# Window attention: value products of both rows at once, own half picked by two projection products; maxima turned in V's bank; V ahead of fc2

## The chip, the core and the metric

The kernel is one program on one core of a Trainium2 chip, whose engines run side by side and meet only at semaphores: TensorE (PE in the rows; PEld is its weight loads), VectorE (DVE), ScalarE (ACT), GpSimd (POOL) and SyncE (SP), which issues DMAs. The metric is device time in microseconds (us) for one execution. All arithmetic is float32.

## The reference, cut to what matters

The input is x of (4, 16, 512, 512). Layer 0 is a block of window attention with an MLP, layer 1 ten steps of a surface flow, layers 2 and 3 two residual pairs of 3x3 convolutions. The change touches layer 0 alone:

```python
x = x + depthwise_conv3x3(x, pos_w) + pos_b            # 16 channels
y = affine(x)                                          # windows of 8x8 = 64 tokens
q, k, v = split(y @ qkv_w.T + qkv_b)                   # 2 heads of 8 channels
out = softmax(q * 8 ** -0.5 @ k.T) @ v
x = x + (out @ proj_w.T + proj_b)
x = x + gelu(affine2(x) @ fc1_w.T + fc1_b) @ fc2_w.T + fc2_b
```

## The kernel before

`attention_stage` does layer 0 and is over before the other layers begin. It cuts the image into 256 **chunks**. A chunk is 8 window rows of 16 channels, which fill the 128 partitions, by 8 windows (WC) of 64 tokens (N), so its main tiles are 128 x 512. Two neighbouring window rows are a **row group** of 32 partitions; there are four (RG), and r is 0 or 1 for the row inside one.

The stage is software-pipelined over slots: one function `slot` on each engine issues, in an order written out by hand, the work of the chunks i-3 to i+2. Each engine runs its own copy in order and waits at semaphores. TensorE's loop holds 20 slots (`every_slot(pe, slot, 5)`), those of ScalarE and VectorE hold 4. One slot of TensorE, with the lines of the profile:

- `scores` of chunk i, first half of the windows (L204), 16 products into the four banks `ps_w`. It waits for `exp_done`: ScalarE must have read the previous contents with its second exponential (L354).
- `values` of chunk i-1, row groups 0 and 1 (L247). For every window, row r and row group one product writes 32 rows by 64 columns of `ps_o`. The stationary operand is `vx`, in which the other row's columns are zero, so that the two products of r = 0 and 1 add up in the same place: 32 products in a call, two calls in a slot.
- `project` of chunk i-2 (L319): one 128 x 512 product with the block-diagonal `w_proj` into bank 0 of `ps_mm`.
- `scores`, second half (L204), which waits for VectorE's first maximum (L483); `values`, row groups 2 and 3.
- `fc1` of chunk i-2 (L275), which waits for the second maximum (L483) because it overwrites `ps_w`.
- `turn_max` (L214): a transpose of the maxima into a bank of its own, `ps_t`; VectorE copies it out (L491). Then `sums` (L260), the denominators.
- `turned`, first half (L228, L234): transposed scores less their maxima. `query` (L283) and `key` (L289) of chunk i+1 into banks 1 and 0 of `ps_mm`. `turned`, second half, which waits for ScalarE's first exponential.
- `fc2` of chunk i-2 (L310) into bank 0, once ScalarE has read the key there (L373); last `value` of chunk i+1 (L298), 16 products into bank 1.

ScalarE's slot is: copy V to `vx` (L386), the output rows (L415), a table load (L423), gelu of i-2 (L404), a table load (L425), logarithm and exponential for the reciprocals (L395, L397), exponential of half 0 (L354), split of Q (L363) and K (L373), exponential of half 1 (L354). VectorE's slot is: maximum of half 0 (L483), `residual` (L508), maximum of half 1, two convolution taps (L469), the copy of the maxima (L491), two more taps and their end (L475), `divide` of i-1 (L500: `ps_o` times the reciprocals into `o_sb`), the first five taps of the next chunk (L464, L469), `finish` of i-2 (L517).

A product stands in the trace as two matmul records and two weight loads.

Of the kernel before, what the change touches and what calls it, by code (L numbers as in the profile page):

```python
# [11 lines left out]
ALU = mybir.AluOpType  # L12
ACT = mybir.ActivationFunctionType
# [4 lines left out]
def attention_stage(nc, x, dst, wt, DST_PAD=2):  # L18

    P = 128  # L20
# [15 lines left out]
    with ExitStack() as ctx:  # L36
        def sb(n, shape):
            return ctx.enter_context(nc.sbuf_tensor("att_" + n, shape, F32))
# [4 lines left out]
        def psum(n, shape):  # L43
            return ctx.enter_context(nc.psum_tensor("att_" + n, shape, F32))
# [3 lines left out]
        qkv_raw, qkv_al = sb("qkv_raw", [P, 3, P]), sb("qkv_al", [P, 3, P])  # L48
        fc1_raw, fc1_al = sb("fc1_raw", [P, RG, P]), sb("fc1_al", [P, RG, P])
        w_qkv, w_fc1 = sb("w_qkv", [P, 3, P]), sb("w_fc1", [P, RG, P])  # L50
        w_proj, w_fc2 = sb("w_proj", [P, P]), sb("w_fc2", [P, RG, P])
        ident = sb("ident", [P, P])
        vec = sb("vec", [P, 24])
        pos_w, pos_b = vec[:, 0:9], vec[:, 9:10]
# [8 lines left out]
        xs = sb("xs", [P, 4, T])  # L63
        qx = sb("qx", [P, 2, WC, 2, N])
        kx = sb("kx", [P, 2, WC, HEADS, N])
        vx = sb("vx", [P, 2, 2, WC, RG, 2, HEADS, HD])
        mx = sb("mx", [P, RG, 32])
        mx_t = sb("mx_t", [P, P])
        minus = sb("minus", [P, WC, P])
# [1 line left out]
        pick = sb("pick", [P, 2, P // RG])  # L71
        rec = sb("rec", [P, T])
        b_out = sb("b_out", [P, 1])
        o_sb = sb("o", [P, T])
        x2 = sb("x2", [P, 2, T])
        hid = sb("hid", [P, 2, RG, T])
        y_sb = sb("y", [P, T])
        out_rows = sb("out_rows", [P, 2, WS, 2 * CW])

        ps_w = psum("w", [P, RG, T])  # L80
        ps_t = psum("t", [P, T])[:, 0:P]
        ps_o = psum("pv", [P, T])
        ps_mm = psum("m", [P, 2, T])
        ps_m = [ps_mm[:, k, :] for k in range(2)]

        w_in, setup, w_made, w_ready = sem("w_in"), sem("setup"), sem("w_made"), sem("w_ready")
# [14 lines left out]
        def wait(eng, s, value):  # L101

            if not isinstance(value, int) or value > 0:
                eng.wait_ge(s, value)
# [16 lines left out]
        def after(eng, *users):  # L121

            for s, c in users:
                if there(c):
                    eng.wait_ge(s, c + 1)
                    return
# [47 lines left out]
        def _(pe):  # L174
# [8 lines left out]
                pe.matmul(ps_mm[:, 0, k:k + 1], qkv_raw[:, k, :], beta1, start=True, stop=True)  # L183
            pe.matmul(ps_mm[:, 0, 3:4], fc1_raw[:, 0, :], beta2, start=True, stop=True).then_inc(w_made, 1)
            pe.wait_ge(w_ready, 1)
            pe.matmul(ps_mm[:, 0, 4:5], w_proj[:, :], b_qkv[:, 2:3], start=True, stop=True).then_inc(w_made, 1)
            pe.wait_ge(w_ready, 2)

            WH = WC // 2
# [18 lines left out]
            def turn_max(i):  # L208

                if not there(i):  # L210
                    return
                pe.wait_ge(max_done, i * 2 + 2)
                wait(pe, mx_copied, i)
                pe.transpose(ps_t[:, :], mx[:, :, :].rearrange("p g k -> p (g k)"), ident[:, :]).then_inc(mx_turned, 1)  # L214

            def turned(i, par, half):
# [20 lines left out]
            def values(i, par, p):  # L237
                if not there(i):
                    return
                if p == 0:  # L240
                    pe.wait_ge(exp_done, i * 2 + 2)
                    pe.wait_ge(v_split, i + 1)
                    wait(pe, o_done, i)
                for w in range(WC):
                    for r in range(2):
                        for rg in (2 * p, 2 * p + 1):
                            mm = pe.matmul(ps_o[32 * rg:32 * rg + 32, w * N:(w + 1) * N],  # L247
                                           vx[:, par, r, w, rg].rearrange("p a h d -> p (a h d)"),
                                           pt[:, par, rg, w, r * N:(r + 1) * N], start=(r == 0), stop=(r == 1))
                mm.then_inc(pv_made[p], 1)  # L250

            def sums(i, par):
# [25 lines left out]
            def query(i, turn4):  # L278
                if not there(i):
                    return  # L280
                pe.wait_ge(conv_step, (i + 1) * STEPS_OF_CONV)
                after(pe, (v_split, i - 1))
                pe.matmul(ps_m[1], w_qkv[:, 0, :], xs[:, turn4, :], start=True, stop=True).then_inc(q_made, 1)  # L283

            def key(i, turn4):
# [17 lines left out]
            def fc2(i, par):  # L303

                if not there(i):
                    return
                pe.wait_ge(gelu_done, i + 1)
                after(pe, (k_split, i + 3), (rec_made, i + 1), (x2_done, i))
                for j in range(RG):
                    mm = pe.matmul(ps_mm[32 * j:32 * j + 32, 0, :], w_fc2[:, j, 32 * j:32 * j + 32], hid[:, par, j, :],  # L310
                                   start=True, stop=True)
                mm.then_inc(f2_made, 1)

            def project(i):
                if not there(i):
                    return
                pe.wait_ge(o_done, i + 1)
                after(pe, (y_done, i - 1), (k_split, i + 2))
                pe.matmul(ps_m[0], w_proj[:, :], o_sb[:, :], start=True, stop=True).then_inc(proj_made, 1)  # L319

            def slot(i, turn4):
                par = turn4 % 2
                o = 1 - par
                scores(i, par, 0)
                values(i - 1, o, 0)
                project(i - 2)
                scores(i, par, 1)
                values(i - 1, o, 1)
                fc1(i - 2, par)
                turn_max(i)  # L330
                sums(i - 1, o)
                turned(i, par, 0)
                query(i + 1, (turn4 + 1) % 4)
                key(i + 1, (turn4 + 1) % 4)
                turned(i, par, 1)
                fc2(i - 2, par)
                value(i + 1, (turn4 + 1) % 4)

            every_slot(pe, slot, 5)

# [1 line left out]
        def _(act):  # L342
# [34 lines left out]
            def split_v(i, par):  # L377
                if not there(i):
                    return
                act.wait_ge(v_made, i + 1)  # L380
                wait(act, pv_made[1], i - 1)
                for h in range(HEADS):
                    hp = slice(N * h, N * h + N)
                    vp = ps_mm[hp, 1, :].rearrange("p (w g r d) -> p w g r d", w=WC, g=RG, r=2)
                    for r in range(2):
                        last = act.activation(vx[hp, par, r, :, :, r, h, :], vp[:, :, :, r, :], ACT.Copy)  # L386
                last.then_inc(v_split, 1)

            def reciprocals(i):
# [44 lines left out]
        @block.vector  # L434
        def _(dve):
            dve.memset(mx[:, :, :], 0.0)
            dve.memset(vx[:].rearrange("p a b c d e f g -> p (a b c d e f g)"), 0.0).then_inc(setup, 1)
            dve.wait_ge(w_in, 16 * 9)
            dve.tensor_scalar(qkv_al[:, :, :], qkv_raw[:, :, :], alpha1, None, ALU.mult)
            dve.tensor_scalar(fc1_al[:, :, :], fc1_raw[:, :, :], alpha2, None, ALU.mult).then_inc(setup, 1)  # L440
# [52 lines left out]
            def divide(i):  # L493
                if not there(i):
                    return
                dve.wait_ge(rec_made, i + 1)
                dve.wait_ge(pv_made[0], i + 1)
                dve.wait_ge(pv_made[1], i + 1)
                wait(dve, proj_made, i)
                dve.tensor_tensor(o_sb[:, :], ps_o[:, :], rec[:, :], ALU.mult).then_inc(o_done, 1)  # L500

            def residual(i, par, turn4):

# [32 lines left out]
def attention_weights(a):  # L536

    import numpy as np
    C, WR, HID = 16, 8, 64
    f = np.float32  # L540

    def blocks(m):

        i, o = m.shape
        z = np.zeros((WR, i, WR, o), m.dtype)
        for r in range(WR):
            z[r, :, r, :] = m
        return z.reshape(WR * i, WR * o)

    def tile(v):  # L550
        return np.tile(np.asarray(v).reshape(-1), 128 // np.asarray(v).size).reshape(128, 1)

    qkv = a["qkv_w"]
    p = np.arange(128)
    row = (p // C) % 2
    head = (p // (C // 2)) % 2
    scale = (C // 2) ** -0.5
    vec = np.concatenate(
        [np.tile(a["pos_w"].reshape(C, 9), (WR, 1)), tile(a["pos_b"]), tile(a["alpha1"]), tile(a["beta1"]), tile(a["alpha2"]),
         tile(a["beta2"])] + [tile(a["qkv_b"][C * k:C * k + C]) for k in range(3)] +  # L560
        [tile(a["proj_b"]), tile(a["fc1_b"]), tile(a["fc2_b"])] +
        [np.where(row == r, scale, 0).astype(f).reshape(128, 1) for r in range(2)] +
        [np.where(head == h, 1, 0).astype(f).reshape(128, 1) for h in range(2)], axis=1).astype(f)
    fc2 = blocks(np.ascontiguousarray(a["fc2_w"].T)).reshape(WR * HID // 128, 128, 128).transpose(1, 0, 2)
    return dict(
        color=np.stack([blocks(a["color1"]), blocks(a["color2"])], axis=1),
        qkv=np.stack([blocks(np.ascontiguousarray(qkv[C * k:C * k + C].T)) for k in range(3)], axis=1),
        fc1=blocks(np.ascontiguousarray(a["fc1_w"].T)).reshape(128, 4, 128),
        proj=blocks(np.ascontiguousarray(a["proj_w"].T)),
        fc2=np.ascontiguousarray(fc2),  # L570
        ident=np.eye(128, dtype=f),
        minus=np.where((p % 32)[:, None, None] == 2 * np.arange(8)[None, :, None] + (p // 64)[None, None, :], -1, 0).astype(f),
        pick=np.stack([(((p[:, None] // 64) == (np.arange(32) // 8) % 2) & (np.arange(32) // 16 == r)).astype(f)
                       for r in range(2)], axis=1),
        vec=vec)
# [855 lines left out]
```

## Time and profile before

| | us |
|---|---|
| median of 3 runs | 28650.5 (28632.8 to 28668.2) |
| the profiled execution | 28647.7, its span 28645.9 |
| attention stage | from the start to about 5250 |
| TensorE busy over the whole span | 26744.7 (93%) |

The attention stage is the first seven of the forty slices of the page; after it come the surface flow and the convolutions, which the change leaves alone. A merged line of a timeline gives the start, the duration from the first to the last of its instructions, how many there are, and in brackets the idle time of the engine ahead of it with what ended it. The end of a matmul is modelled, so starts are the surer numbers.

### The profile page before, as it was taken

What the parts mean: (1) busy time and instruction counts of PE and PEld (TensorE: products, weight loads), DVE (VectorE), ACT (ScalarE), POOL (GpSimd) and SP (SyncE); (2) the same over time, 40 slices, a digit from 0 to 9 for tenths busy, and PEclk for the clock granted to TensorE, in tenths of its full rate; (3) what the DMA queues carried; (4) which work ended last, traced back from release to release, by engine and by line L of the source; (5) the groups of instructions that cost most, each with busy time, mean ns of one, the idle gap of its engine ahead of it and who ended that gap; (6) DMA issues with size and microseconds to landing.
All of it is one profiled execution on the core that took longest, in us unless ns stands there. A gap on an engine that the chain in (4) does not pass through costs nothing. (4 is left out here: it accounts for less than half of the span.)

```text
span 28645.9 us, 827717 instructions
## 1 busy us (share of the span) xinstructions
PE 26744.7 (93%) x334232; PEld 12655.2 (44%) x334232; DVE 23740.9 (83%) x26151; ACT 23103.3 (81%) x23277; POOL 8975.8 (31%) x9524
## 2 busy tenths in 40 slices
PE   8999999999989989998999899999989998999799
PEld 5666666444334433443434344334434443444455
DVE  6666666799989989998999899889989998999222
ACT  6666666799989989998999899889989998999111
POOL 0000000244434434443444344434434443444000
PEclk9999999999999999999999999999999999999899
DMA  1111111699999999999999999999999999999654
GB/s 33 32 32 32 32 32 32 126 176 176 178 177 176 177 177 178 176 176 178 176 176 178 178 176 176 180 175 176 176 178 175 176 176 179 176 176 176 119 106 90
DMA packets 1942097, 4147.74 MB, mean 145 GB/s; under 512 B 590960, under 2 KB 722544, under 8 KB 1938160
## 3 DMA queue, kind: packets, MB, share of 16 engines
q0 software_dynamic: 1196800, 3565.77, 70.6%
q1 hardware_dynamic: 701424, 469.69, 8.2%
q10 hardware_dynamic: 41088, 67.14, 1.1%
q8 instruction: 2726, 44.66, 0.6%
q14 instruction: 59, 0.48, 0.0%
HBM read 294.41 MB, written 201.33 MB: 17 GB/s over the span
## 5 line engine op out<-in xcount | busy, mean ns | idle before, releaser
L872 PE MATMUL surf_ps<-surf_u,surf_matf 64*64 64x512 f32 x184960 | 20141.9, 593 | 1129.8 <-ACT surf_pq L895 703.1
L872 PEld LDWEIGHTS surf_ps<-surf_u,surf_matf 64*64 64x64 f32 x184960 | 8316.3, 133 | 12956.2 <-issue 12897.1
L929 ACT ACTIVATE surf_p2q<-surf_pq 128x2048 f32<-128x2048 f32 x1360 | 2599.9, 1912 | 1484.5 <-DVE surf_pq L1016 1484.5
L969 POOL DMA_DIRECT2D surf_u<-surf_ds x4080 | 3458.4, 1156 | 954.0 <-issue 483.3
L962 POOL DMA_DIRECT2D surf_p2q<-surf_p2q x1360 | 1161.3, 854 | 7773.6 <-DVE surf_Ha L1038 7280.0
L956 POOL DMA_DIRECT2D surf_nK<-surf_B x1360 | 1236.4, 909 | 6884.4 <-ACT surf_B L933 6870.3
L1051 DVE SCALAR_TENSOR_TENSOR surf_rH<-surf_Hc,surf_dt_ab,surf_rH 128x1024 f32<-128x1024 f32 x1360 | 1744.0, 1282 | 1454.7 <-DMA surf_Hc<-surf_m 1045.0
L981 POOL DMA_DIRECT2D surf_Hc<-surf_Ha x1360 | 2187.1, 1608 | 351.2 <-DVE surf_Hc L1060 344.2
L975 POOL DMA_DIRECT2D surf_Hc<-surf_m x1360 | 1466.2, 1078 | 1648.1 <-DMA surf_Hc<-surf_Ha 1521.8
L1027 DVE SCALAR_TENSOR_TENSOR surf_nK<-surf_Ac,surf_Cc 128x1024 f32<-128x1024 f32 x1360 | 1666.8, 1226 | 180.6
L1021 DVE SCALAR_TENSOR_TENSOR surf_ds<-surf_nK,surf_dt_ab,surf_rH 128x1024 f32<-128x1024 f32 x1360 | 1731.0, 1273 | 0.3
L1060 DVE SCALAR_TENSOR_TENSOR surf_Hc<-surf_p2q,surf_Cc 128x1024 f32<-128x1024 f32 x1360 | 1666.6, 1225 | 24.0
L404 ACT ACTIVATE att_hid<-att_w,att_b_fc 128x2048 f32<-128x2048 f32 x256 | 503.7, 1968 | 1464.9 <-PE att_w L275 1464.9
L1038 DVE SCALAR_TENSOR_TENSOR surf_Ha<-surf_p2q,surf_Ac 128x1024 f32<-128x1024 f32 x1360 | 1656.0, 1218 | 5.2 <-ACT surf_p2q L929 5.2
L1016 DVE TENSOR_SCALAR surf_pq<-surf_pq 128x2048 f32<-128x2048 f32 x1360 | 1651.9, 1215 | 6.2 <-ACT surf_pq L901 6.2
L1031 DVE TENSOR_TENSOR surf_m<-surf_m,surf_Bc 128x1024 f32<-128x1024 f32 x1360 | 1656.8, 1218 | 0.0
L1064 DVE SCALAR_TENSOR_TENSOR surf_m<-surf_pq 128x1024 f32<-128x1024 f32 x1360 | 1656.7, 1218 | 0.0
L1048 DVE TENSOR_TENSOR surf_nK<-surf_nK,surf_rK 128x1024 f32<-128x1024 f32 x1360 | 1655.2, 1217 | 1.3 <-DMA surf_nK<-surf_B 1.3
L895 ACT ACTIVATE surf_pq<-surf_ps 128x1024 f32<-128x1024 f32 x1360 | 1363.6, 1003 | 331.6 <-PE surf_ps L872 331.6
L483 DVE TENSOR_REDUCE att_mx<-att_w 128x32 f32<-128x2048 f32 x512 | 1173.3, 2292 | 520.8 <-PE att_w L204 520.8
L469 DVE SCALAR_TENSOR_TENSOR att_acc<-att_xin,att_vec,att_acc 128x512 f32<-128x512 f32 x2048 | 1535.1, 750 | 54.3
L901 ACT ACTIVATE surf_pq<-surf_ps 128x1024 f32<-128x1024 f32 x1360 | 1391.3, 1023 | 116.2 <-PE surf_ps L872 98.2
(107 smaller groups left out, 39009.4 us busy)
## 6 DMA issues: line engine op xcount, KB each, us to landing
surf_p2q<-surf_p2q POOLq DMA_DIRECT2D x1360, 512.0 KB, 11.3
surf_Hc<-surf_Ha POOLq DMA_DIRECT2D x1360, 512.0 KB, 13.4
surf_nK<-surf_B POOLq DMA_DIRECT2D x1360, 512.0 KB, 9.6
surf_Hc<-surf_m POOLq DMA_DIRECT2D x1360, 512.0 KB, 11.5
surf_u<-surf_ds POOLq DMA_DIRECT2D x1360, 256.0 KB, 5.7
surf_u<-surf_ds POOLq DMA_DIRECT2D x2720, 128.0 KB, 9.6
att_xin<-in_x SPq DMA_DIRECT2D x2048, 41.2 KB, 2.1
attended<-att_out_rows SPq DMA_DIRECT2D x1024, 64.0 KB, 2.0
```

Source lines behind the costliest of these rows:

```text
L872: mm = pe.matmul(ps[out, t, :], matf[rows, mat, :], u[rows, k, t, off + 2:off + 2 + W], start=(i == 0), stop=(i == len(taps) - 1))
L929: act.activation(both(p2q2, par), both(pq, par), ACT.Square).then_inc(squared["pq"], 1)
L969: pool.dma_start(u[rows, k, t, 2:W + 2].rearrange("p a w -> p (a w)"), ds[found, t, :], accum_op=ALU.add).then_inc(u_added, 16)
L981: pool.dma_start(buf("Hc", par), buf("Ha", par), accum_op=ALU.add).then_inc(t12_done, 16)
L1021: dve.scalar_tensor_tensor(out=buf("ds", o), in0=buf("nK", o), scalar=minus_alpha, in1=buf("rH", o), op0=ALU.mult, op1=ALU.add).then_inc(s ...
L1027: dve.scalar_tensor_tensor(out=buf("nK", o), in0=buf("Ac", o), scalar=-1.0, in1=buf("Cc", o), op0=ALU.mult, op1=ALU.mult).then_inc(ac_done, 1)
L1031: dve.tensor_tensor(buf("m", o), buf("m", o), buf("Bc", o), ALU.mult).then_inc(m_done, 1)
L1038: dve.scalar_tensor_tensor(out=buf("Ha", par), in0=buf("q2", par), scalar=1.0, in1=buf("Ac", par), op0=ALU.add, op1=ALU.mult).then_inc(t1_ ...
L1048: dve.tensor_tensor(buf("nK", par), buf("nK", par), buf("rK", par), ALU.mult).then_inc(k_made, 1)
L1051: dve.scalar_tensor_tensor(out=buf("rH", par), in0=buf("Hc", par), scalar=beta, in1=buf("rH", par), op0=ALU.mult, op1=ALU.mult).then_inc(h ...
L1060: dve.scalar_tensor_tensor(out=buf("Hc", par), in0=buf("p2", par), scalar=1.0, in1=buf("Cc", par), op0=ALU.add, op1=ALU.mult).then_inc(t2_ ...
L1064: dve.scalar_tensor_tensor(out=buf("m", par), in0=buf("pc", par), scalar=-2.0, in1=buf("qc", par), op0=ALU.mult, op1=ALU.mult).then_inc(pq ...
```

## The change

1. `values`: one product for a window and row group in place of two. Its stationary operand holds V of both rows, without zeros, and its moving operand both rows' probabilities, 128 columns; the result holds all four pairs of rows, of which two are meant. `ps_o` and `o_sb` grow from 512 to 1024 columns, `vx` halves.
2. `project`: two products of 512 columns that add up, one for each r. `w_proj` has a plane for each r in which the other row's input channels are zero, so the unwanted pairs drop out.
3. `divide` covers 1024 columns, the reciprocals read twice.
4. `split_v`: one ScalarE copy per head, 64 x 512, in place of two of 64 x 256.
5. `ps_t` loses its bank, which `ps_o` needs, and becomes the first 128 columns of bank 1 of `ps_mm`. So `turn_max` waits for `v_split` of its own chunk, and `query` for `mx_copied`.
6. On TensorE, `value` of i+1 is issued ahead of `fc2` of i-2.

```diff
-        vx = sb("vx", [P, 2, 2, WC, RG, 2, HEADS, HD])
+        vx = sb("vx", [P, 2, WC, RG, 2, HEADS, HD])
-        o_sb = sb("o", [P, T])
+        o_sb = sb("o", [P, WC, 2, N])
-        ps_t = psum("t", [P, T])[:, 0:P]
-        ps_o = psum("pv", [P, T])
+        ps_o = psum("pv", [P, WC, 2, N])
         ps_mm = psum("m", [P, 2, T])
+        ps_t = ps_mm[:, 1, 0:P]
...
                 pe.wait_ge(max_done, i * 2 + 2)
-                wait(pe, mx_copied, i)
+                pe.wait_ge(v_split, i + 1)
...
                 for w in range(WC):
-                    for r in range(2):
-                        for rg in (2 * p, 2 * p + 1):
-                            mm = pe.matmul(ps_o[32 * rg:32 * rg + 32, w * N:(w + 1) * N],
-                                           vx[:, par, r, w, rg].rearrange("p a h d -> p (a h d)"),
-                                           pt[:, par, rg, w, r * N:(r + 1) * N], start=(r == 0), stop=(r == 1))
+                    for rg in (2 * p, 2 * p + 1):
+                        mm = pe.matmul(ps_o[32 * rg:32 * rg + 32, w].rearrange("p r n -> p (r n)"),
+                                       vx[:, par, w, rg].rearrange("p r h d -> p (r h d)"), pt[:, par, rg, w, :], start=True, stop=True)
...
-                after(pe, (v_split, i - 1))
+                after(pe, (mx_copied, i - 1))
                 pe.matmul(ps_m[1], w_qkv[:, 0, :], xs[:, turn4, :], start=True, stop=True).then_inc(q_made, 1)
...
-                pe.matmul(ps_m[0], w_proj[:, :], o_sb[:, :], start=True, stop=True).then_inc(proj_made, 1)
+                for r in range(2):
+                    last = pe.matmul(ps_m[0], w_proj[:, r, :], o_sb[:, :, r, :], start=(r == 0), stop=(r == 1))
+                last.then_inc(proj_made, 1)
...
                 turned(i, par, 1)
+                value(i + 1, (turn4 + 1) % 4)
                 fc2(i - 2, par)
-                value(i + 1, (turn4 + 1) % 4)
...
-                    vp = ps_mm[hp, 1, :].rearrange("p (w g r d) -> p w g r d", w=WC, g=RG, r=2)
-                    for r in range(2):
-                        last = act.activation(vx[hp, par, r, :, :, r, h, :], vp[:, :, :, r, :], ACT.Copy)
+                    last = act.activation(vx[hp, par, :, :, :, h, :].rearrange("p w g r d -> p (w g) r d"),
+                                          ps_mm[hp, 1, :].rearrange("p (k r d) -> p k r d", r=2, d=HD), ACT.Copy)
...
-                dve.tensor_tensor(o_sb[:, :], ps_o[:, :], rec[:, :], ALU.mult).then_inc(o_done, 1)
+                dve.tensor_tensor(o_sb[:, :, :, :], ps_o[:, :, :, :],
+                                  rec[:, :].rearrange("p (w n) -> p w n", n=N).unsqueeze(2).to_broadcast([P, WC, 2, N]), ALU.mult).then_inc(o_done, 1)
```

TensorE's instructions from the end of `turned` to `fc1`, before (att_m is `ps_mm`, att_pv `ps_o`, att_w `ps_w`; L310 is fc2, L298 V, L204 scores, L247 values, L319 the projection):

```order
L234 MATMUL att_w<-att_mx_t,att_minus 128x128 x4
L310 MATMUL att_m<-att_hid,att_w_fc 32x512 x4
L298 MATMUL att_m<-att_w_qkv,att_xs 64x64 x16
L204 MATMUL att_w<-att_kx,att_qx 128x128 x16
L247 MATMUL att_pv<-att_pt,att_vx 32x64 x32
L319 MATMUL att_m<-att_o,att_w_proj 128x512
L204 MATMUL att_w<-att_kx,att_qx 128x128 x16
L247 MATMUL att_pv<-att_pt,att_vx 32x64 x32
L275 MATMUL att_w<-att_x,att_w_fc 128x512 x4
```

The same stretch of the changed kernel, where L298 is still V and L310 fc2, L206 are the scores, L248 the values, L320 the projection:

```order
L236 MATMUL att_w<-att_mx_t,att_minus 128x128 x4
L298 MATMUL att_m<-att_w_qkv,att_xs 64x64 x16
L310 MATMUL att_m<-att_hid,att_w_fc 32x512 x4
L206 MATMUL att_w<-att_kx,att_qx 128x128 x16
L248 MATMUL att_pv<-att_pt,att_vx 32x128 x16
L320 MATMUL att_m<-att_o,att_w_proj 128x512 x2
L206 MATMUL att_w<-att_kx,att_qx 128x128 x16
L248 MATMUL att_pv<-att_pt,att_vx 32x128 x16
L275 MATMUL att_w<-att_x,att_w_fc 128x512 x4
```

V and fc2 have changed places, the values are half as many products of twice the columns, and the projection is two products. In VectorE's order no instruction has moved, but `divide` is larger. Before:

```order
L475 TENSOR_TENSOR att_xs<-att_acc,att_xin 128x512
L500 TENSOR_TENSOR att_o<-att_pv,att_rec 128x512
L464 TENSOR_SCALAR att_acc<-att_xin,att_vec 128x512
L469 SCALAR_TENSOR_TENSOR att_acc<-att_xin,att_vec,att_acc 128x512 x4
L517 SCALAR_TENSOR_TENSOR att_y<-att_m,att_vec,att_x 128x512
```

The same stretch of VectorE in the changed kernel:

```order
L476 TENSOR_TENSOR att_xs<-att_acc,att_xin 128x512
L501 TENSOR_TENSOR att_o<-att_pv,att_rec 128x1024
L465 TENSOR_SCALAR att_acc<-att_xin,att_vec 128x512
L470 SCALAR_TENSOR_TENSOR att_acc<-att_xin,att_vec,att_acc 128x512 x4
L519 SCALAR_TENSOR_TENSOR att_y<-att_m,att_vec,att_x 128x512
```

Only the shape of the second row differs.

## Rows read from the trace of the kernel before

**Rows 1.** Windows, attention: stretch, length, busy (x) PE PEld DVE ACT POOL, clock, DMA.
```profile
76.40:5192.00 5115.60, 4683.92 (x98330) 3145.86 (x98330) 3533.22 (x4028) 3498.47 (x4026) 0.00 (x0) 0.99 0.19 32
```
**Rows 2.** Timeline of ScalarE, gelu alone: start, duration, and idle time before.
```profile
2701.58 1.97 ACT L404 ACTIVATE att_hid<-att_w,att_b_fc 128x2048 f32<-128x2048 f32 x1 [5.49 <-PE att_w L275]
...
2882.34 1.97 ACT L404 ACTIVATE att_hid<-att_w,att_b_fc 128x2048 f32<-128x2048 f32 x1 [5.49 <-PE att_w L275]
```
**Rows 3.** Timeline of ScalarE, one slot from gelu to the second exponential.
```profile
3002.90 1.97 ACT L404 ACTIVATE att_hid<-att_w,att_b_fc 128x2048 f32<-128x2048 f32 x1 [5.49 <-PE att_w L275]
...
3007.34 1.87 ACT L354 ACTIVATE att_pt<-att_w 128x2048 f32<-128x2048 f32 x1
...
3010.42 1.46 ACT L373 ACTIVATE att_kx<-att_m,att_k_bias,att_vec 128x512 f32<-128x512 f32 x2
3011.74 1.90 ACT L354 ACTIVATE att_pt<-att_w 128x2048 f32<-128x2048 f32 x1
```
**Rows 4.** Timeline of TensorE, same slot, from the turned scores on.
```profile
3009.26 0.50 PE L228 MATMUL att_w<-att_qx,att_kx 32*128 32x128 f32 x8 [0.27 <-ACT att_pt L354]
...
3010.70 0.40 PE L228 MATMUL att_w<-att_qx,att_kx 32*128 32x128 f32 x8
3010.93 0.40 PE L234 MATMUL att_w<-att_mx_t,att_minus 32*128 32x128 f32 x8
3012.02 1.07 PE L310 MATMUL att_m<-att_hid,att_w_fc 128*32 128x512 f32 x8 [0.69 <-ACT att_kx L373]
...
3014.10 1.17 PE L204 MATMUL att_w<-att_kx,att_qx 32*128 32x128 f32 x32
3015.20 1.98 PE L247 MATMUL att_pv<-att_pt,att_vx 128*32 128x64 f32 x64
3017.11 1.12 PE L319 MATMUL att_m<-att_o,att_w_proj 128*128 128x512 f32 x2
3018.17 1.17 PE L204 MATMUL att_w<-att_kx,att_qx 32*128 32x128 f32 x32
...
3021.76 1.14 PE L275 MATMUL att_w<-att_x,att_w_fc 32*128 32x512 f32 x8 [0.50 <-DVE att_mx L483]
```
**Rows 5.** Timeline of VectorE, same slot.
```profile
3007.47 0.69 DVE L500 TENSOR_TENSOR att_o<-att_pv,att_rec 128x512 f32<-128x512 f32 x1 [1.87 <-ACT att_rec L397]
...
3013.15 0.75 DVE L517 SCALAR_TENSOR_TENSOR att_y<-att_m,att_vec,att_x 128x512 f32<-128x512 f32 x1 [1.38 <-PE att_m L310]
3015.34 2.29 DVE L483 TENSOR_REDUCE att_mx<-att_w 128x32 f32<-128x2048 f32 x1 [1.44 <-PE att_w L204]
3018.28 0.75 DVE L508 SCALAR_TENSOR_TENSOR att_x<-att_m,att_b_out,att_xs 128x512 f32<-128x512 f32 x1 [0.65 <-PE att_m L319]
3019.41 2.29 DVE L483 TENSOR_REDUCE att_mx<-att_w 128x32 f32<-128x2048 f32 x1 [0.38 <-PE att_w L204]
```
**Rows 6.** Timeline of the weight loads (PEld): sums, and the second half of key.
```profile
3003.47 0.13 PEld L260 LDWEIGHTS att_m<-att_pt,att_pick 128*32 128x32 f32 x4 [0.30 <-issue]
3003.90 0.13 PEld L260 LDWEIGHTS att_m<-att_pt,att_pick 128*32 128x32 f32 x4 [0.30 <-issue]
```
**Rows 7.** Waits in a window of the attention stage: total us, times, longest.
```profile
PEld att_w L204 <- DVE att_mx L483: 0.8, 1, 0.8
```
**Rows 8.** Groups by line and shape, 1000 to 5000 us.
```profile
L386 ACT ACTIVATE att_vx<-att_m 64x256 f32<-64x256 f32 x784 | 253.9, 372 | 118.2 <-PE att_m L298 115.9
L395 ACT ACTIVATE att_rec<-att_m 128x512 f32<-128x512 f32 x196 | 117.0, 597 | 2.2
```
**Rows 9.** One line of the later stage, L1048: duration ns min/median/max.
```profile
L1048 DVE TENSOR_TENSOR surf_nK<-surf_nK,surf_rK x1360: 1211/1217/1226, 5328.5 to 26569.3; 128x1024 f32<-128x1024 f32 x195
```
**Rows 10.** Timeline of TensorE where its loop of 20 slots starts over.
```profile
613.59 2.09 PE L204 MATMUL att_w<-att_kx,att_qx 32*128 32x128 f32 x32 [3.53 <-issue]
615.61 3.63 PE L247 MATMUL att_pv<-att_pt,att_vx 128*32 128x64 f32 x64
...
620.51 1.17 PE L204 MATMUL att_w<-att_kx,att_qx 32*128 32x128 f32 x32
```

More of the change, by code:

```diff
@@ L50, in attention_stage @@
         w_qkv, w_fc1 = sb("w_qkv", [P, 3, P]), sb("w_fc1", [P, RG, P])
-        w_proj, w_fc2 = sb("w_proj", [P, P]), sb("w_fc2", [P, RG, P])
+        w_proj, w_fc2 = sb("w_proj", [P, 2, P]), sb("w_fc2", [P, RG, P])
         ident = sb("ident", [P, P])
@@ L185, in _ @@
             pe.wait_ge(w_ready, 1)
-            pe.matmul(ps_mm[:, 0, 4:5], w_proj[:, :], b_qkv[:, 2:3], start=True, stop=True).then_inc(w_made, 1)
+            for r in range(2):
+                last = pe.matmul(ps_mm[:, 0, 4:5], w_proj[:, r, :], b_qkv[:, 2:3], start=(r == 0), stop=(r == 1))
+            last.then_inc(w_made, 1)
             pe.wait_ge(w_ready, 2)
@@ L318, in project @@
                 after(pe, (y_done, i - 1), (k_split, i + 2))
-                pe.matmul(ps_m[0], w_proj[:, :], o_sb[:, :], start=True, stop=True).then_inc(proj_made, 1)
+                for r in range(2):
+                    last = pe.matmul(ps_m[0], w_proj[:, r, :], o_sb[:, :, r, :], start=(r == 0), stop=(r == 1))
+                last.then_inc(proj_made, 1)
             def slot(i, turn4):
@@ L436, in _ @@
             dve.memset(mx[:, :, :], 0.0)
-            dve.memset(vx[:].rearrange("p a b c d e f g -> p (a b c d e f g)"), 0.0).then_inc(setup, 1)
+            dve.memset(vx[:].rearrange("p a b c d e f -> p (a b c d e f)"), 0.0).then_inc(setup, 1)
             dve.wait_ge(w_in, 16 * 9)
@@ L568, in attention_weights @@
         fc1=blocks(np.ascontiguousarray(a["fc1_w"].T)).reshape(128, 4, 128),
-        proj=blocks(np.ascontiguousarray(a["proj_w"].T)),
+        proj=np.stack([np.where((row == r)[:, None], blocks(np.ascontiguousarray(a["proj_w"].T)), 0) for r in range(2)],
+                      axis=1).astype(f),
         fc2=np.ascontiguousarray(fc2),
```

## The prediction

> **What bounds the kernel now.** The change touches only the attention stage, so I started at its windows. In [rows 1] TensorE is busy 4683.9 of 5115.6 us, 92%, VectorE 69% and ScalarE 68%, at a granted clock of 0.99 (the 2.4 GHz level). A share of 92% invites the reading that every nanosecond of TensorE counts; but it says only that its waits are short, and the question is whether they stand in a chain. So next I took the period. In [rows 2] gelu starts at 2701.58 and, nine slots later, at 2882.34: 180.76 / 9 = 20.08 us a slot, and ScalarE waits 5.49 us ahead of each gelu. 256 chunks by 20.08 us are 5140 us, nearly the whole stage.
>
> Then one slot, engine by engine, looking for the ring of work that closes on itself:
>
> - ScalarE starts gelu at 3002.90 and goes without a bracketed wait until its second exponential ends at 3011.74 + 1.90 = 3013.64 [rows 3].
> - That exponential frees the score banks. The scores of the next chunk start at 3014.10 [rows 4], 0.46 us later. They are not late through ScalarE: where TensorE really waits for an exponential (the first ends at 3007.34 + 1.87 = 3009.21 in [rows 3], the next product starts at 3009.26 in [rows 4]) the hand-over takes 0.05 us. So 0.41 us are lost because TensorE is still at fc2 and V, after it stood 0.69 us for the key split [rows 4].
> - Scores to first maximum: the reduction starts at 3015.34 and takes 2.29, ends 3017.63 [rows 5]. The second scores could start at 3017.68, yet start at 3018.17 [rows 4]. Between stand the values (3015.20, 1.91 us to the next start) and the projection (3017.11, 1.06 us).
> - Second scores to second maximum (3019.41 + 2.29 = 3021.70 in [rows 5]), fc1 at 3021.76 [rows 4], and gelu again.
>
> Once round: 10.74 us of ScalarE, two scores, two maxima, fc1, and of TensorE's other work only what lies between the first and the second scores. The second values, the denominators, Q, K, V and fc2 are beside the ring; TensorE waits 0.50 us before fc1 and 0.27 before the turned scores [rows 4]. What counts is thus: when the first scores can start, and how long TensorE takes from there to the second.
>
> One row must be read with care. [rows 7] puts 0.8 us of idle weight loading ahead of L204 down to the first maximum. But that maximum ended at 3017.63, 0.54 us before the start. The projection takes two passes of its 512 columns, 0.43 us each by the weight loads of other 512-column passes at 3003.47 and 3003.90 [rows 6]. From 3017.11 this runs to 3017.97, with the first weight load ahead of it to about 3018.1. TensorE itself is the last to come here.
>
> **The change, part by part, in us a slot.**
>
> Projection, on the ring. It becomes two products, four passes for two: 2 x 0.43 = **+0.86**. The least is this, since columns can't go faster than the pass in [rows 6]; the most is the whole present piece once more, 1.06, if a weight load is laid bare each time. I take 0.86: the loads in [rows 6] go on under the running pass.
>
> First values, on the ring. 64 records of 64 columns become 32 of 128, in sets of two column groups side by side. Now they take 1.91, 32 sets of 0.056 and a start of 0.1 (an estimate: the projection has 1.06 for 0.86 of passes, so 0.2 at most). For 128 columns the nearest row is the turned scores: from 3010.70 to 3010.93, 8 records of 128 columns, four at a time, so 0.11 a set [rows 4]. 16 x 0.11 + 0.10 = 1.86: **-0.05**. The columns are as many as before (32 x 64 = 16 x 128), and the array was already streaming. Bounds: 0 to -0.10. The second values save as much beside the ring, which only lengthens the wait before fc1.
>
> The Trainium skill speaks otherwise. Its page "TensorEngine Tiling (Array Packing)", section "Instruction Overhead", gives every matmul about 60 cycles of overhead and lets one column cost what 60 do. By it, halving the number of products would pay well. The trace does not agree: a set takes 0.056 us, and 64 of the 512 columns that pass in 0.43 us [rows 6] take 0.054.
>
> V ahead of fc2, on the ring through the start of the scores. V needs the query split and not the key split, so it can go once the turned scores are through, at about 3010.93 + 0.23 = 3011.2. fc2 and V together take 2.08 now (3012.02 to 3014.10 in [rows 4]), about half each; fc2 then starts near 3012.3, by when the key split is over (3010.42 + 1.46 = 3011.88 in [rows 3]), and ends near 3013.3. The scores then wait for the exponential alone and start at 3013.69: **-0.41** of the 0.83 that TensorE gains. The rest becomes a new wait at L206. Bounds -0.35 to -0.45 (a hand-over of 0.11 or 0.01).
>
> Hidden edits:
> - `divide` 0.69 becomes 1.22, the duration of 128 x 1024 in [rows 9]. It delays the taps by 0.53, and VectorE waits 1.38 before `finish` [rows 5]. `finish` itself comes 0.28 later or so, since fc2 follows V, and ends before 3014.3; the next maximum starts at about 3014.9. Without that cover 0.53 a slot.
> - `split_v`: two ScalarE copies of 512 for four of 256. With 0.37 for one of 256 and 0.60 for 512 columns from PSUM [rows 8], 1.2 against 1.3 now, and 5.49 us of waiting follow [rows 2]. Nothing.
> - The maxima in V's bank. `turn_max` stands after fc1, 8 us after V was made, and `split_v` ends within 2 us; `query` stands behind the turned scores, which themselves wait for L491. Neither new wait comes last, so nothing queued behind them on TensorE is delayed.
> - Set-up: one more small product, half the memset. Below 1 us in all.
>
> Sum: 0.86 - 0.05 - 0.41 = **+0.40** a slot, 20.08 to about 20.48; 256 slots give **+102 us**.
>
> Where TensorE's loop starts over, 11 times, it stands 3.53 us and is then slow: from scores to second scores 613.59 to 620.51, 6.92 against 4.07 [rows 4, 10]. The values there last 3.56 for 1.91. If that is the supply of instructions, half as many products help, up to 1.65 - and an earlier end of the slot's work may start the loop's jump sooner. I take -1.2 a time, of 0 to -3: -13 us.
>
> Total +89 us on the profiled 28647.7, 28737; that execution was 2.8 below the median, so **28740**. The terms' ends: 0.86 - 0.10 - 0.45 = 0.31, or +79, less 33: +46, 28696. Above: 1.06 - 0.35 = 0.71, +182: 28832.
>
> **The rivals.**
>
> - *Loads laid bare in the projection.* Each of the four passes shows its load; the ring gets 1.06 - 0.05 - 0.41 = +0.60, +154 - 13 = +141 us, 28792. For it: 128-column loads are the longest here. Against: [rows 6].
> - *The projection is hidden, and the result is faster.* If the second scores really wait for the first maximum, as [rows 7] says, 0.49 us of the longer projection are free. The slot changes by 0.86 - 0.49 - 0.05 - 0.41 = -0.09, or -23 - 13 = -36 us, 28615. It decides once TensorE is free more than 0.05 us before 3018.17. Against it: 0.54 us between the maximum's end and the start.
> - *A fixed cost for each product.* If half the products take half the time, the first values fall by 0.95: 0.86 - 0.95 - 0.41 = -0.50, -128 - 13, 28510. Against: 0.056 us a set now. This is also what the Trainium skill's rule in "Instruction Overhead" would lead to, here not borne out by [rows 4].
> - *The gain at the loop's start is large* (-3 each) and the terms lie at their low ends: 28696, no measurable change.
>
> **How the numbers follow.** About 0.2% (57 us) is what measurement of this kernel tells from none: the bounds are 28593 and 28708. Forecast 0.72, of which 0.12 fall below 28708; loads laid bare 0.10; hidden projection 0.08 (half of it within 0.2%); fixed cost 0.04; large loop gain 0.06. Slower 0.60 + 0.10 = 0.70; same 0.12 + 0.06 + 0.04 = 0.22; faster 0.08. The range 28680 to 28815 leaves out the two faster rivals and the far tail.
>
> **What would show it.** In the profile after: gelu every 20.48 us; the projection (L320) 1.9 us from the next scores; the values (L248) 1.86; the first scores 0.05 after the second exponential, with a wait on it of about 0.4; the wait before fc2 gone and that before fc1 near 0.6; `divide` 1.22 with VectorE still waiting before `finish`. Wrong if the second scores start as soon after the first maximum as 0.05 us, if the values take under 1.5, or if another engine's wait (finish, copy of the maxima) has come into the ring.

## The result, and the profile after

The changed kernel takes 28730.1 us (median of 9 runs, 28706.9 to 28751.8) against 28642.1 of the kernel before beside it (median of 9, 28621.2 to 28668.2): a ratio of 1.003, 95% interval 1.0019 to 1.0040. It is slower, by 88 us, which is 0.3%. The forecast was 28740 with a range of 28680 to 28815, and 89 us more than before.

The same stretch of the attention stage, in the columns of [rows 1] (stretch, length, busy time and count of PE, PEld, DVE, ACT, POOL, granted clock, DMA):

```profile
76.40:5192.00 5115.60, 4791.57 (x81281) 3102.06 (x81281) 3601.83 (x3954) 3370.47 (x3458) 0.00 (x0) 1.00 0.18 31
```

TensorE is busier than in [rows 1] (94% for 92%) with a sixth fewer instructions in the same stretch, and the stage takes longer: gelu, nine slots apart as in [rows 2], went from 20.08 to (2896.72 - 2712.25) / 9 = 20.50 us a slot, and the wait ahead of it from 5.49 to 6.72 (the 11.12 in the first of these rows stands behind a start of TensorE's loop).

```profile
2712.25 1.97 ACT L405 ACTIVATE att_hid<-att_w,att_b_fc 128x2048 f32<-128x2048 f32 x1 [11.12 <-PE att_w L275]
...
2896.72 1.97 ACT L405 ACTIVATE att_hid<-att_w,att_b_fc 128x2048 f32<-128x2048 f32 x1 [6.72 <-PE att_w L275]
```

One slot of ScalarE and of TensorE, as in [rows 3] and [rows 4] (L356 is the exponential, L298 V, L310 fc2, L206 the scores, L248 the values, L320 the projection):

```profile
3028.53 1.90 ACT L356 ACTIVATE att_pt<-att_w 128x2048 f32<-128x2048 f32 x1
```

```profile
3028.05 1.15 PE L298 MATMUL att_m<-att_w_qkv,att_xs 128*64 128x64 f32 x32
3029.13 1.07 PE L310 MATMUL att_m<-att_hid,att_w_fc 128*32 128x512 f32 x8
3030.48 1.17 PE L206 MATMUL att_w<-att_kx,att_qx 32*128 32x128 f32 x32 [0.29 <-ACT att_pt L356]
3031.59 1.94 PE L248 MATMUL att_pv<-att_pt,att_vx 128*32 128x128 f32 x32
3033.46 1.98 PE L320 MATMUL att_m<-att_o,att_w_proj 128*128 128x512 f32 x4
3035.37 0.84 PE L206 MATMUL att_w<-att_kx,att_qx 32*128 32x128 f32 x20
```

The scores wait for the exponential (3028.53 + 1.90 = 3030.43) and start 0.05 us behind it, where they came 0.46 behind before. The new wait is 0.29 us where about 0.4 was forecast; the one before fc2 is gone, and the one before fc1 is 0.54. The values take 1.87 us to the next start for 1.91, the projection 1.91 for 1.06. So the second scores come 4.89 us after the first, 4.07 before.

The same slot of VectorE, as in [rows 5] (L501 is `divide`, L519 `finish`, L484 the maxima):

```profile
3024.26 1.23 DVE L501 TENSOR_TENSOR att_o<-att_pv,att_rec 128x1024 f32<-128x1024 f32 x1 [1.88 <-ACT att_rec L398]
...
3030.26 0.75 DVE L519 SCALAR_TENSOR_TENSOR att_y<-att_m,att_vec,att_x 128x512 f32<-128x512 f32 x1 [1.18 <-PE att_m L310]
3031.72 2.29 DVE L484 TENSOR_REDUCE att_mx<-att_w 128x32 f32<-128x2048 f32 x1 [0.71 <-PE att_w L206]
```

`divide` has grown from 0.69 to 1.23 us, and VectorE still waits 1.18 before `finish` and 0.71 before the first maximum. The first maximum ends at 3034.01, and the second scores start 1.36 us later: what they wait for is TensorE.

### The profile page after: what moved, and what is told of

The parts are those of the page before. It is cut to its first block and busy times, and to the rows that moved or that the text cites. A ratio compares the mean times of both kernels' runs of the same rounds, so it can differ in the third digit from the quotient of the medians.

```text
span 28740.5 us, 795466 instructions
## 1 busy us (share of the span) xinstructions
PE 26936.9 (94%) x318362; PEld 12710.3 (44%) x318362; DVE 23872.1 (83%) x26151; ACT 23045.0 (80%) x22765; POOL 8992.9 (31%) x9524
## 5 line engine op out<-in xcount | busy, mean ns | idle before, releaser
L904 ACT ACTIVATE surf_pq<-surf_ps 128x1024 f32<-128x1024 f32 x1360 | 1391.4, 1023 | 130.0 <-PE surf_ps L875 109.3
L918 ACT ACTIVATE surf_rK<-surf_rK 128x1024 f32<-128x1024 f32 x1360 | 1438.4, 1058 | 43.1
```

## The experiments

The theory on trial is the **ring**: gelu to second exponential on ScalarE (about 10.7 us), then first scores, first values and projection on TensorE or the first maximum on VectorE, whichever ends last, second scores, second maximum, fc1. Its rivals are that TensorE's whole work is the bound, that the projection is hidden behind the first maximum, and that a product costs a fixed amount. Every kernel was timed in three rounds beside the kernel before, and each ratio is against the runs of its own rounds, whose median was 28627.4 for the first four experiments and 28641 to 28642 for the others. So the ratios and the slots compare better than the medians. A **regular slot** in the table at the end of this section is the mean interval between two gelus in the profiled run, without those in which TensorE's loop starts over (11 with 20 slots) and without the last two; the starts are given apart, as their mean over the median slot.

**The swap alone.**

```diff
-                fc2(i - 2, par)
                 value(i + 1, (turn4 + 1) % 4)
+                fc2(i - 2, par)
```

> The kernel before with edit 6 alone: V ahead of fc2. Ring theory: the first scores then wait for the second exponential, 0.41 us earlier a slot and no more: gelu every 19.67 us for 20.085, the scores 0.05 us behind the exponential, about 105 to 115 us less, 28530 to 28540. Rival, TensorE's whole work is the bound: all of the 0.69 us wait before fc2 comes back, 19.35 a slot, 28455. Rival, the swap is worth nothing by itself: 28642.

28520.8 us, ratio 0.9961 (0.9947 to 0.9975), the regular slot 19.68. Only 0.40 of the wait of 0.69 before fc2 comes back, as the ring has it; the rest is a new wait at the scores:

```profile
3027.59 1.07 PE L310 MATMUL att_m<-att_hid,att_w_fc 128*32 128x512 f32 x8
3028.95 1.17 PE L204 MATMUL att_w<-att_kx,att_qx 32*128 32x128 f32 x32 [0.29 <-ACT att_pt L354]
3030.05 1.98 PE L247 MATMUL att_pv<-att_pt,att_vx 128*32 128x64 f32 x64
3031.96 1.12 PE L319 MATMUL att_m<-att_o,att_w_proj 128*128 128x512 f32 x2
```

TensorE's whole work as the bound (19.35 a slot, 28455) is out. The swap by itself is a gain of 0.4%.

**The changed kernel without the swap.** fc2 ahead of V again.

```diff
-                value(i + 1, (turn4 + 1) % 4)
                 fc2(i - 2, par)
+                value(i + 1, (turn4 + 1) % 4)
```

> The changed kernel with fc2 ahead of V again, all else as changed. Ring theory: 20.50 + 0.41 = 20.91 us a slot, some 105 us over the changed kernel, 28835. If the swap earned nothing beside the longer projection: 28730. It also tells what the loop's start owes to the order: the 11 long intervals were 25.06 us on average with the swap and 25.81 before the change.

28849.4 us, ratio 1.0078 (1.0061 to 1.0094), slot 20.905. Merging and the doubled projection, without the swap, cost 0.82 us a slot. The swap is worth 0.40 here too: the two edits add up.

**The doubled projection alone.** Two products with the two planes of the weights, over the old `o_sb`; `w_proj` gets its planes as in the change.

```diff
-                pe.matmul(ps_m[0], w_proj[:, :], o_sb[:, :], start=True, stop=True).then_inc(proj_made, 1)
+                for r in range(2):
+                    last = pe.matmul(ps_m[0], w_proj[:, r, :], o_sb[:, :], start=(r == 0), stop=(r == 1))
+                last.then_inc(proj_made, 1)
```

> The kernel before with the projection alone as two products (one for each half of the weights, over the same moving operand); values and order as before. Ring theory: 0.86 us a slot more, 20.945, about 28862. Rival, the second scores wait for the first maximum anyway: 0.49 of it is hidden, 0.37 more a slot, 28737. Rival, every weight load laid bare: 1.06 more, 28913.

28885.0 us, ratio 1.0087 (1.0069 to 1.0104), slot 20.94, +0.86. In this kernel's timeline (L322 is the projection) it takes 1.92 us to the next scores:

```profile
3016.97 1.98 PE L322 MATMUL att_m<-att_o,att_w_proj 128*128 128x512 f32 x4
3018.89 1.17 PE L206 MATMUL att_w<-att_kx,att_qx 32*128 32x128 f32 x32
```

Nothing of it is hidden, although [rows 7] had put the idle time at this place down to the first maximum. Nor are the weight loads laid bare: that would be 2.12. The run time alone could not say this, since 28885 lies midway between 28862 and the 28913 of bare loads; the slot (20.94, not 21.14) and the row do.

**The changed kernel with one projection product.** The other row's half of the projection is left out.

```diff
-                for r in range(2):
-                    last = pe.matmul(ps_m[0], w_proj[:, r, :], o_sb[:, :, r, :], start=(r == 0), stop=(r == 1))
-                last.then_inc(proj_made, 1)
+                pe.matmul(ps_m[0], w_proj[:, 0, :], o_sb[:, :, 0, :], start=True, stop=True).then_inc(proj_made, 1)
```

> The changed kernel with only the first of its two projection products, so the other row's half of the projection is left out. Ring theory: 0.86 us a slot less, 19.64, about 28510; the second scores start 1.06 us behind the projection and are still 0.45 us later than the first maximum allows. It gives what merged values and swap are worth without their price: 0.45 us a slot against the kernel before.

28518.2 us, ratio 0.9958 (0.9941 to 0.9974), slot 19.64. That is 0.86 below the changed kernel, and 0.04 below the swap alone: merging the values, free of its price, gives 0.04 us a slot. The output of this kernel is not the layer's; it serves for timing.

**Windows of the first values moved behind the second scores.** If the ring is right, its TensorE piece can be shortened without less work: the values' order among themselves is free. K is 2, 4 or 3 windows of row groups 0 and 1; the changed kernel has no loop over r here.

```diff
-                for w in range(WC):
+                EARLY = WC - K
+                todo = [(w, 0) for w in range(EARLY)] if p == 0 else [(w, 0) for w in range(EARLY, WC)] + [(w, 1) for w in range(WC)]
+                for w, g in todo:
                     for r in range(2):
-                        for rg in (2 * p, 2 * p + 1):
+                        for rg in (2 * g, 2 * g + 1):
```

Two windows, without the swap:

> The kernel before with the two windows moved and no swap. Ring theory: 0.45 us a slot less, 19.63, about 28520, the two edits add up. Rival, the reading that the second scores wait for the first maximum: unchanged, 28630.

28540.9 us, 0.9963 (0.9949 to 0.9978), slot 19.635, -0.45.

Two windows and the swap:

> The kernel before with V ahead of fc2 and with the last two windows of the first values (8 of 32 products) issued behind the second scores. Ring theory: first values 1.45 us for 1.91; the second scores start 3.62 us behind the first, just when the first maximum allows (3.58); the second values grow to 2.4 and still end before the second maximum. 0.45 us a slot less than the swap alone, 19.22, about 28410. Rival, TensorE's own work now binds (it is busy 18.6 us a slot and its waits are short): no more than 0.2 gained, 28470. Rival, the maximum is what the second scores wait for: nothing gained, 28521.

28402.2 us, 0.9912 (0.9895 to 0.9928), slot 19.23. The second scores start 3.62 us after the first (L249 are the values, L321 the projection, L485 the maximum, which ends at 3006.94):

```profile
3003.41 1.17 PE L204 MATMUL att_w<-att_kx,att_qx 32*128 32x128 f32 x32 [0.29 <-ACT att_pt L356]
3004.51 1.53 PE L249 MATMUL att_pv<-att_pt,att_vx 128*32 128x64 f32 x48
...
3005.98 1.12 PE L321 MATMUL att_m<-att_o,att_w_proj 128*128 128x512 f32 x2
3007.03 1.17 PE L204 MATMUL att_w<-att_kx,att_qx 32*128 32x128 f32 x32
3008.14 2.24 PE L249 MATMUL att_pv<-att_pt,att_vx 128*32 128x64 f32 x80
...
3010.62 1.14 PE L277 MATMUL att_w<-att_x,att_w_fc 32*128 32x512 f32 x8 [0.24 <-DVE att_mx L485]
```

TensorE's piece and VectorE's are now equal to 0.04 us.

Four windows and the swap:

> The same with four windows moved. Ring theory: the second scores can start no sooner than 3.58 us behind the first, since the first maximum ends then, so nothing more is gained there; the second values take 2.8 us and end 0.35 after the second maximum, so fc1 waits for TensorE. About 19.53 us a slot, 28490: slower than two windows moved. If TensorE's work between the two scores were all that counts: 18.76 a slot, 28300.

28441.5 us, 0.9928 (0.9911 to 0.9944), slot 19.33. The floor is where it was put. The second scores start 3.59 us after the first and now do wait for the maximum:

```profile
3014.42 1.17 PE L204 MATMUL att_w<-att_kx,att_qx 32*128 32x128 f32 x32 [0.29 <-ACT att_pt L356]
3015.53 1.09 PE L249 MATMUL att_pv<-att_pt,att_vx 128*32 128x64 f32 x32
...
3018.01 1.17 PE L204 MATMUL att_w<-att_kx,att_qx 32*128 32x128 f32 x32 [0.34 <-DVE att_mx L485]
3019.11 2.69 PE L249 MATMUL att_pv<-att_pt,att_vx 128*32 128x64 f32 x96
3021.73 1.14 PE L277 MATMUL att_w<-att_x,att_w_fc 32*128 32x512 f32 x8
```

fc1 has lost its bracket and follows the values. The loss against two windows was put too high, at 0.3 a slot, and is 0.10: the second values take 2.62 us, not 2.8, so fc1 is less late.

Three windows moved in the changed kernel:

> The changed kernel with three windows of the first values moved behind the second scores. Ring theory: 0.66 us less between the scores, so the second scores start 4.2 us behind the first (the maximum allows 3.58); behind them 1.10 + 2.53 us of TensorE for 3.58 to the second maximum, so fc1 is 0.05 to 0.1 late. 0.57 to 0.6 a slot less, 19.92, about 28590: it beats the kernel before and stays behind the same move without merged values, since the doubled projection is TensorE's work either way.

28555.2 us, 0.9972 (0.9959 to 0.9984), slot 19.84. All of the 0.66 is gained (20.50 to 19.84), where 0.57 to 0.6 was expected: fc1 is not late, it still waits 0.29 us for the second maximum. The kernel beats the kernel before and is 153 us behind the unmerged values with the same kind of move: the doubled projection is work that has to stand somewhere.

**The length of TensorE's loop.** Two windows, the swap, and `every_slot(pe, slot, 15)` (60 slots) or `every_slot(pe, slot, 1)` (4 slots).

```diff
-            every_slot(pe, slot, 5)
+            every_slot(pe, slot, 15)
```

> The swap and two windows moved, with TensorE's loop of 60 slots in place of 20: it starts over 3 times, not 11. In the run with 20 slots each such interval of gelu was 4.4 us longer than the others (23.60 against 19.22). If that is a price for every start of the loop: 8 fewer, 35 us less, 28367. If it comes with the number of instructions that pass (the supply of new code), the same is paid in other places or in longer pieces: 28402.

28369.1 us, 0.9908 (0.9891 to 0.9925). The median is 33 us below that of the 20 slots (0.9912), but the two intervals overlap almost wholly, so the run times don't decide. The traces do: from the first gelu to the last it takes 4909.3 us for 4943.7, which is 34 less, and the regular slot is the same within 0.01. The price is for each start. This is the lowest median of the study.

> The same with TensorE's loop of 4 slots: 60 starts over. If each costs 4.4 us as with 20 slots: 49 more, 215 us more, 28617. If a loop that short can be held ready and starts over at no cost: 11 x 4.4 = 48 us less, 28354.

28603.3 us, 0.9987 (0.9977 to 0.9997). A loop of 4 slots does not start over for nothing either: 60 of its intervals are long, by 3.4 us on average.

| kernel | median us | regular slot | loop start, over a slot | starts |
|---|---|---|---|---|
| before | 28642.1 | 20.08 | 5.75 | 11 |
| changed | 28730.1 | 20.50 | 4.57 | 11 |
| swap alone | 28520.8 | 19.68 | 4.65 | 11 |
| changed, no swap | 28849.4 | 20.905 | 5.24 | 11 |
| doubled projection alone | 28885.0 | 20.94 | 5.78 | 11 |
| changed, one projection product | 28518.2 | 19.64 | 4.58 | 11 |
| two windows | 28540.9 | 19.635 | 6.20 | 11 |
| two windows, swap | 28402.2 | 19.23 | 4.38 | 11 |
| four windows, swap | 28441.5 | 19.33 | 3.94 | 11 |
| changed, three windows | 28555.2 | 19.84 | 3.53 | 11 |
| two windows, swap, loop of 60 | 28369.1 | 19.24 | 3.55 | 3 |
| two windows, swap, loop of 4 | 28603.3 | 19.22 | 3.43 | 60 |

## Why the prediction was right, and where it was not

**The ring** is shown. Three edits that each change one of its pieces moved the slot by what the piece changed (+0.86, -0.40, -0.45), singly and together, and the move stopped paying at the 3.58 us that VectorE needs.

**The projection**, forecast +0.86: +0.86 alone, +0.86 in the changed kernel.

**The first values**, -0.05: 1.87 for 1.91 in the trace, and -0.04 in both differences (20.905 - 20.94, 19.64 - 19.68). The rival of a fixed cost for each product would have taken 0.95 off; half the products brought a twenty-fourth of that. That the term came within 0.01 is partly luck: the two rows it was taken from lie 0.23 us apart for two sets, and with 0.115 a set in place of the rounded 0.11 the same sum gives 1.94, or +0.03. The Trainium skill's "Instruction Overhead" in "TensorEngine Tiling (Array Packing)" gives each matmul about 60 cycles of overhead and lets one column take as long as 60. Taken as a cost added to each product, as the rival had it, it does not fit these rows; taken as a least duration it is not tested by them, since these products have 64 and 128 columns.

**The swap**, -0.41: -0.40. The larger part of what TensorE gains turned into a wait for the exponential, as named.

**The hidden projection** was the rival on the other side, and [rows 7] spoke for it. It is out: the piece grew by 0.86 us and the slot by as much. The wait belonged to TensorE's own queue of work, since the maximum had ended 0.54 us earlier. In the kernel with four windows moved the wait is real, and then the bracket stands in the PE rows as well (0.34), not in those of the weight loads alone.

**The hidden edits** cost nothing in a regular slot: 0.86 - 0.04 - 0.40 = 0.42, with the 0.04 of the values' own rows, is all of the 0.41 by which it grew. They were not tried one by one.

**The start of the loop**: the size was right (-1.2 forecast, 5.75 to 4.57 measured), the main reason was not, and that the size fitted is luck. It rested on the supply of instructions, by which half as many products shorten the slow values after the stop. They are not shorter. In the changed kernel, after such a stop:

```profile
626.34 2.09 PE L206 MATMUL att_w<-att_kx,att_qx 32*128 32x128 f32 x32 [3.20 <-issue]
628.37 3.63 PE L248 MATMUL att_pv<-att_pt,att_vx 128*32 128x128 f32 x32
631.92 2.23 PE L320 MATMUL att_m<-att_o,att_w_proj 128*128 128x512 f32 x4
```

From first to last they take 3.63 us, 32 records of 128 columns, and 3.63 in [rows 10], 64 records of 64. The windows of the kernel before say why (the third number from the right is the granted clock):

```profile
605.00:610.00 5.00, 4.16 (x104) 3.08 (x104) 3.30 (x5) 4.53 (x6) 0.00 (x0) 1.00 0.45 80
610.00:613.50 3.50, 0.06 (x3) 0.00 (x0) 0.00 (x0) 3.21 (x6) 0.00 (x0) 0.92 0.37 61
613.60:619.00 5.40, 5.40 (x96) 5.17 (x96) 2.29 (x1) 0.00 (x0) 0.00 (x0) 0.50 0.21 34
619.20:620.50 1.30, 1.30 (x4) 0.47 (x2) 0.00 (x0) 0.00 (x0) 0.00 (x0) 0.78 0.06 13
```

After 3.5 us without work TensorE runs at a granted clock of 0.50, the 1.2 GHz level, for 5.4 us and is then back at 1.00. So this start of the loop costs the stop and then columns at half speed. The others differ in how long the low clock lasts. Behind the next stop of the kernel before (3.77 us) it is 0.51 from 1023 to 1026 and 1.00 from 1026 to 1029; and at two of the 11 starts of the changed kernel, after stops of 3.22 and 2.81 us, it stays at 1.00 and the second scores come after the usual 4.89 us.

Over all 11 starts, the second scores follow the first 1.93 us later than in a regular slot in the kernel before and 1.88 in the changed one, so the slow columns give next to nothing of the saving. It comes from what the prediction named beside its main reason and gave no size of its own, an earlier end of the slot's work. TensorE's last product before the stop ends 0.52 us behind the second exponential in the kernel before and 0.24 ahead of it in the changed one; of these 0.76 us a regular slot gains 0.41 as well, and 0.35 is left. The stop itself shrinks from 3.67 to 2.91 us on average, 0.76 more. The swap alone does the same (5.75 to 4.65, stops of 3.00). Why a stop is shorter when TensorE has ended earlier is open. Merging and the doubled projection without the swap give 5.24, with stops of 3.48 and slow columns of 1.61; the doubled projection alone 5.78, with 3.61 and 2.02. Whether that difference is the merge's doing or that of the one execution profiled of each is open too.

The loop of 4 slots shows the two costs apart: at 28 of its 60 starts the second scores come after the usual 3.62 us, and these cost 2.2 to 3.1 us over a slot; at the other 32 they come after 5.2, and these cost 3.8 to 4.6. The granted clock is 1.00 from 445.3 to 449.5, behind a stop of the first kind, and 0.66 from 283 to 288, behind one of the second.

The sum, on the profiled runs: the 11 intervals of gelu with a start of the loop shrank from 25.81 to 25.06 us, -8 in all, and the 244 others, with the two short ones at the end, grew from 20.04 to 20.46, +102. That is 94, and the spans differ by 28740.5 - 28645.9 = 94.6. The slots outside the loop are dearer wherever the scores wait for the exponential (20.61 against 20.48 in the changed kernel, 20.10 against 20.07 before): there the scores start 0.14 us behind the exponential, not 0.05 (151.70 for 149.66 + 1.90 in the changed kernel). That was in no term; for some 13 slots it is about 1 us.

## What to carry to other kernels

Before giving work to an engine that is busy 92% of the time, find the ring that sets the period and ask whether the work stands in it. Here one reordering, which leaves TensorE's work as it was, won 0.4%, and moving eight small products past one wait won as much, while halving the number of products won 0.04 us a slot. Before merging small products, count passes times columns before and after: here they were equal, and the second projection product that the merge needed cost twenty times what the merge gave. A wait that a profile puts down to one engine has to be checked against when that engine ended.

## What the runs showed of the hardware

A start of TensorE's loop stops it for 2.4 to 4.0 us in these traces (3.53 in [rows 10], 3.20 in the changed kernel), and a body of 4 slots does not avoid it. The granted clock was 0.50 for the 5.4 us after the stop shown, for less after others, and 1.00 throughout after some. By the traces, 8 starts fewer were worth 34 us, about 4.3 each.
